# A gated-scan mixer and two local-attention layers on one core: norm shift moved into biases, small steps moved from GpSimd to VectorE and ScalarE, and the loop over passes written out

## The reference

```
q, k = l2norm(q) * qs, l2norm(k) * ksc          # per head, over 64 features
q, k = rotary_xpos(q, k)                        # q*cos*scale + rotate_half(q)*sin*scale, k with 1/scale
x = x + local_attention(q, k, v) @ wo
h = shift_token(x)                              # second half of the features from the token before
h = (h - mu) / jnp.sqrt(var + 1e-05) * lg + lb
a, g = jnp.split(h @ w1 + b1, 2, axis=-1)
x = x + (a * jax.nn.gelu(g)) @ w2 + b2
```

## Time and profile before

| | us |
|---|---|
| median of 3 runs | 432.49 (432.48 to 435.87) |
| span of the profiled execution, first to last instruction | 431.7 |
| TensorE busy | 351.5 (81%) |
| VectorE busy | 321.6 (74%) |
| GpSimd busy | 301.1 (70%) |
| ScalarE busy | 280.8 (65%) |
| weight loads of TensorE, beside its products | 287.5 (67%) |

### The profile page before, as it was taken

One profiled execution on the slowest core, in us unless ns is written; L12 is line 12 of the kernel. 1 busy time (PEld: TensorE's weight loads), 2 busy tenths in 40 slices (PEclk: granted clock), 3 DMA queues, 4 the chain that ended last, 5 costly groups with the idle time before them and its releaser, 6 DMA issues.

```text
span 431.7 us, 11030 instructions
## 1 busy us (share of the span) xinstructions
PE 351.5 (81%) x3832; PEld 287.5 (67%) x3832; DVE 321.6 (74%) x751; ACT 280.8 (65%) x844; POOL 301.1 (70%) x247
## 2 busy tenths in 40 slices
PE   1573055899999899999999999999999989988781
PEld 1352034677778687778777887788778867766561
DVE  6889964787689767966796788688869877954653
ACT  3552263688678677867786788678777868764430
POOL 2200419899999889988998699869887988780222
PEclk9996557999999999999999999999999999998966
DMA  7700042412142125112511342043204220220110
GB/s 262 225 0 0 13 125 60 110 27 50 46 118 56 32 55 141 30 30 64 133 32 33 105 94 51 15 121 76 62 3 117 65 53 2 57 57 2 24 49 25
DMA packets 42373, 28.29 MB, mean 66 GB/s; under 512 B 21668, under 2 KB 36566, under 8 KB 42326
## 3 DMA queue, kind: packets, MB, share of 16 engines
q1 hardware_dynamic: 42325, 27.68, 24.4%
HBM read 13.51 MB, written 3.15 MB: 39 GB/s over the span
## 4 chain that ended last, share of the span: by engine, by line
PE 37%; DVE 23%; POOL 19%; issue 11%; ACT 7%; DMA 1%; SPq 1%; POOLq 1%; DVEq 0%; ACTq 0%
POOL rn L507 7%; PE bank L726 5%; POOL rot L552 4%; PE bank L771 4%; DVE rot_sin L1153 4%; PE upper L708 3%; DVE rot_cos L1153 3%; POOL rot L541 3%; ACT probs L902 3%; PE bank L650 2%; PE bank L763 2%; DVE normed L1052 2%; PE upper L659 2%; PE bank L590 2%; DVE neg_max L1201 2%
## 5 line engine op out<-in xcount | busy, mean ns | idle before, releaser
L902 ACT ACTIVATE probs<-upper,neg_max 128x128 f32<-128x128 f32 x256 | 90.4, 369 | 48.5 <-DVE neg_max L1201 48.4
L507 POOL TENSOR_TENSOR rn<-floored,minus_half 128x16 f32<-128x16 f32 x32 | 93.8, 2930 | 2.7
L541 POOL TENSOR_TENSOR rot<-rot_cos,rot_sin 128x512 f32<-128x512 f32 x32 | 40.9, 1277 | 44.3 <-issue 23.6
L1201 DVE TENSOR_REDUCE neg_max<-upper 128x4 f32<-128x512 f32 x64 | 43.1, 684 | 27.5 <-PE upper L708 27.4
L552 POOL TENSOR_TENSOR rot<-rot,rn 128x1024 f32<-128x1024 f32 x32 | 60.9, 1903 | 2.5
L902 ACT ACTIVATION_READ_ACCUMULATOR probs<-upper,neg_max 128x1 f32 x256 | 53.0, 207 | 0.0
L590 PE MATMUL bank<-wqkv_hi,act_t_hi 128*128 128x512 f32 x96 | 43.3, 452 | 7.9 <-DVE act_t_lo L1140 2.8
L1153 DVE TENSOR_TENSOR rot_cos<-bank,tab 128x512 f32<-128x512 f32 x64 | 43.6, 681 | 2.0 <-PE bank L594 1.9
L1153 DVE TENSOR_TENSOR rot_sin<-bank,tab 128x512 f32<-128x512 f32 x64 | 43.4, 679 | 0.0
L542 POOL TENSOR_TENSOR rot<-rot_cos,rot_sin 128x512 f32<-128x512 f32 x32 | 40.9, 1279 | 0.0
L1160 DVE TENSOR_REDUCE ss<-sq 128x16 f32<-128x1024 f32 x32 | 38.7, 1209 | 2.4 <-ACT sq L944 2.3
(11 more groups left out here) (140 smaller groups left out, 863.7 us busy)
## 6 DMA issues: line engine op xcount, KB each, us to landing
v_mid<-v_tok SPq DMA_DIRECT2D x64, 128.0 KB, 2.3
tab_raw<-tables SPq DMA_DIRECT2D x8, 512.0 KB, 3.4
h_tok<-group_in SPq DMA_DIRECT2D x14, 128.0 KB, 3.5
x_res<-group_in SPq DMA_DIRECT2D x28, 64.0 KB, 1.8
wqkv_raw<-wqkv SPq DMA_DIRECT2D x2, 768.0 KB, 6.8
x_in<-x SPq DMA_DIRECT2D x4, 256.0 KB, 3.6
head_scale<-head_scales SPq DMA_DIRECT2D x8, 128.0 KB, 4.0
group_in<-normed SPq DMA_DIRECT2D x4, 256.0 KB
```

What stands on the lines that cost most here:

```text
L507: pool.tensor_tensor(rn[:, 0:2 * HEADS], floored[:, 0:2 * HEADS], minus_half[:, :], ALU.pow).then_inc(rn_ready, 1)
L541: pool.tensor_tensor(rot[cur.par][:, :, 0:32], rot_cos[:, :, 0:32], rot_sin[:, :, 32:64], ALU.add).then_inc(rot_added, 1)
L902: last = act.activation(probs[:, h, :], s_bank[half][:, (h % 4) * P:(h % 4 + 1) * P], ACT.Exp, bias=neg_max[a.par][:, h:h + 1], accum_out= ...
L1201: dve.tensor_reduce(neg_max[a.par][:, 4 * half:4 * half + 4], src, AX.X, ALU.max, negate=True).then_inc(max_ready, 1)
```

## The change

1. The shift `ln_b` of the norm before the feed-forward leaves the activation of h. Instead `w1^T ln_b` is computed once, by 12 one-column products on TensorE after the mixer, and 12 activations on ScalarE add it to `b1`. With the shift gone, the full copy `h2_t` goes too: `h2_lo` is made by one VectorE instruction that reads PSUM, scales, and subtracts `h2_hi`. TensorE now waits for `h2_lo` before the second half of the first chunk and no longer after it.
2. The floor of the sums of squares leaves GpSimd: `ss` gets a second column that holds the floor, and VectorE takes a maximum over the pair right after `sum_squares`.
3. The carry of 64 keys leaves GpSimd for ScalarE, which takes them straight from PSUM at j = 1.
4. `scale_table` of groups 1 to 7 leaves GpSimd for VectorE, at the end of each position (the four slots of group 0 stay on GpSimd).
5. `place_early` moves from the end of `finish_group` (j = 2) to behind `rotate` of j = 3.
6. All passes are written out; `Fori`, register-valued waits and `settle` are gone.

```diff
-        ss = sb("ss", [P, 2 * HEADS])
+        ss = sb("ss", [P, 2 * HEADS, 2])
...
+        def passes(body, ending):
+            for G in range(-1, LAST - 1):
+                body(G)
+            body(LAST - 1, 2)
             ending()
...
+            pool.memset(ss[:, :, 1], NORM_FLOOR).then_inc(init_done, 1)
...
             def norm_roots(t):
-                pool.wait_ge(ss_ready, t + 1)
-                settle(pool)
-                pool.tensor_scalar(floored[:, 0:2 * HEADS], ss[:, :], NORM_FLOOR, None, ALU.max).then_inc(ss_floored, 1)
+                need(pool, rot_scaled, t)
                 pool.wait_ge(ss_floored, t + 1)
...
-                    if not (number and not 0 <= G < LAST - 1):
-                        scale_table(G + 1, j)
...
-                    if cur.valid and cur.slot == 0 and not (number and G < 0):
-                        pool.wait_ge(k_saved, t)
-                        pool.wait_ge(s_done, 2 * (t - GT + 1))
-                        settle(pool)
-                        if cur.first:
-                            pool.memset(k_t[:, :, 0:WINDOW], 0.0).then_inc(k_carried, 1)
-                        else:
-                            pool.tensor_copy(k_t[:, :, 0:WINDOW], k_t[:, :, GTOK:GTOK + WINDOW]).then_inc(k_carried, 1)
...
+            def project_shifts():
+                pe.wait_ge(w_ffn_in, W_IN)
+                pe.wait_ge(hidden_read, GROUPS)
+                for l in range(DEPTH):
+                    pe.wait_ge(w_big_in[l], 32)
+                    for part in range(2):
+                        for c, (c0, cn) in enumerate(CHUNKS):
+                            at = 6 * l + 3 * part + c
+                            last = pe.matmul(shift_bank[0:cn, at:at + 1], w1_raw[l][:, part * HID + c0:part * HID + c0 + cn],
+                                             lngb[l][:, 1:2], start=True, stop=True)
+                last.then_inc(shift_up, 1)
...
                         if c == 0 and part == 1:
                             if between:
                                 between()
-                            pe.wait_ge(h2t_saved, 2 * F + 2)
-                            settle(pe)
+                            pe.wait_ge(h2_split, F + 1)
                         pe.matmul(b[0:cn, :], w1_hi[layer][:, w], h2_hi[:, :], start=True, stop=False)
                         pe.matmul(b[0:cn, :], w1_lo[layer][:, w], h2_hi[:, :], start=False, stop=False)
-                    if c == 0:
-                        pe.wait_ge(h2_split, F + 1)
-                        settle(pe)
...
+            def shift_biases():
+                act.wait_ge(shift_up, 1)
+                for l in range(DEPTH):
+                    for part in range(2):
+                        for c, (c0, cn) in enumerate(CHUNKS):
+                            at = 3 * part + c
+                            act.activation(b1_sb[l][0:cn, at:at + 1], shift_bank[0:cn, 6 * l + at:6 * l + at + 1], ACT.Identity,
+                                           bias=b1_sb[l][0:cn, at:at + 1]).then_inc(bias_ready, 1)
...
+            def carry_keys(a):
+                if tile(a.t + 1).first:
+                    source = zeros[:, 0:WINDOW].unsqueeze(1).broadcast_to([P, PAIRS, WINDOW])
+                else:
+                    source = kt_bank[:, :].rearrange("p (c t) -> p c t", c=PAIRS)[:, :, P - WINDOW:P]
+                act.copy(k_t[:, :, 0:WINDOW], source).then_inc(k_carried, 1)
...
-                act.activation(dst[:, :], h2t_bank[:, :], ACT.Identity, bias=lngb[l][:, 1:2],
-                               scale=lngb[l][:, 0:1]).then_inc(h2t_saved, 1)
+                act.activation(h2_hi[:, :], h2t_bank[:, :], ACT.Identity, scale=lngb[l][:, 0:1]).then_inc(h2t_saved, 1)
...
+            def scale_table(G, j):
+                dve.wait_ge(tab_in, 32 * (G + 1))
+                dve.tensor_tensor(tab[:, j, :], tab_raw[:, j, :], head_scale[:, :], ALU.mult).then_inc(tab_ready, 1)
...
-                dve.tensor_reduce(ss[:, :], sq[:, :].rearrange("p (h d) -> p h d", h=2 * HEADS), AX.X, ALU.add).then_inc(ss_ready, 1)
+                dve.tensor_reduce(ss[:, :, 0], sq[:, :].rearrange("p (h d) -> p h d", h=2 * HEADS), AX.X, ALU.add).then_inc(ss_ready, 1)
+                dve.wait_ge(ss_ready, a.t + 1)
+                need(dve, rn_ready, a.t)
+                dve.tensor_reduce(floored[:, 0:2 * HEADS], ss[:, :, :], AX.X, ALU.max).then_inc(ss_floored, 1)
...
-                dve.wait_ge(h2t_saved, 2 * (F + 1))
-                dve.tensor_tensor(h2_lo[:, :], h2_t[:, :], h2_hi[:, :].bitcast(F32), ALU.subtract).then_inc(h2_split, 1)
+                dve.wait_ge(h2t_saved, F + 1)
+                dve.scalar_tensor_tensor(h2_lo[:, :], h2t_bank[:, :], lngb[F // GROUPS][:, 0:1], h2_hi[:, :].bitcast(F32),
+                                         ALU.mult, ALU.subtract).then_inc(h2_split, 1)
...
             def finish_group(F, layer):
                 sum_group(F, layer, x_attn)
-                dve.wait_ge(carry_in, 16 * (F + 1))
-                place_early(F + 1)
...
                     if cur.valid:
                         rotate(cur)
+                    if j == 3 and G >= 1:
+                        dve.wait_ge(carry_in, 16 * G)
+                        place_early(G)
...
+                    if 0 <= G < LAST - 1:
+                        scale_table(G + 1, j)
```

More of the change, by code:

```diff
@@ L259, in tile @@
[L259 to L280 removed]
+            if value > 0:
+                eng.wait_ge(s, value)
@@ L299, in link @@
                 self.catch_up()
-            def enter(self):
-                self.start, self.n = self.base + self.n, 0
-            def at(self, i, each):
-                self.base, self.each = self.start + i * each, each
-            def leave(self, times):
-                assert self.n == self.each, f"a pass of the loop has {self.n} steps"
-                self.base, self.n = self.start + times * self.each, 0
         def low_pieces(l):
@@ L384, in load_carry @@
                 need(sp, h2_in, 64 * (F + 1))
-                ends = isinstance(F, int) and F % GROUPS == GROUPS - 1
+                ends = F % GROUPS == GROUPS - 1
                 last = zeros[P - 1:P, 64:128] if ends else x_attn[P - 1:P, GT, 64:128]
-                dst = x_last if isinstance(F, int) and F == LAST - 2 else x_attn
+                dst = x_last if F == LAST - 2 else x_attn
                 sp.dma_start(dst[P - 1:P, 0, 64:128], last).then_inc(carry_in, 16)
@@ L399, in store @@
                     sp.dma_start(by_group(out)[F - GROUPS], y_out[:, :, :]).then_inc(stored, 16)
-                if not (isinstance(F, int) and F == LAST - 1):
+                if F != LAST - 1:
                     need(sp, carry_in, 16 * (F + 1))
@@ L449, in body @@
                         load_carry(G - 1)
-                    if j == 3 and number and G > GROUPS + 1:
+                    if j == 3 and G > GROUPS + 1:
                         store(G - 2, DEPTH - 1)
-                if count == GT and not (number and (G < 1 or G > GROUPS)):
-                    store(G - 1, (G - 1) // GROUPS if number else layer)
+                if count == GT and 1 <= G <= GROUPS:
+                    store(G - 1, (G - 1) // GROUPS)
             def ending():
@@ L787, in body @@
                 for j in range(count):
-                    cur, prev, mid, done, after = (At(G, j, back, layer) for back in range(5))
-                    ffn = j == 2 and not (number and G < 1)
+                    cur, prev, mid, done, after = (At(G, j, back) for back in range(5))
+                    ffn = j == 2 and G >= 1
                     if cur.valid:
@@ L807, in body @@
                         pe.wait_ge(k_saved, prev.t + 1)
-                    if j == 0 and not (number and not 0 <= G < LAST - 1):
+                    if j == 0 and 0 <= G < LAST - 1:
                         transpose_inputs(G + 1)
@@ L1225, in place_early @@
             def place_early(G):
-                if not (isinstance(G, int) and G >= LAST - 1):
+                if G < LAST - 1:
                     dve.wait_ge(xa_ready, GT * G + 2)
@@ L1254, in normalise_out, with body @@
                 last.then_inc(y_normed, 1)
-            def body(G, layer, count=GT):
-                number = isinstance(G, int)
+            def body(G, count=GT):
                 for j in range(count):
-                    cur, prev, mid, done, after = (At(G, j, back, layer) for back in range(5))
-                    norm, ffn = (j == n and not (number and G < 1) for n in (1, 2))
-                    final = j == 3 and number and G > GROUPS
+                    cur, prev, mid, done, after = (At(G, j, back) for back in range(5))
+                    norm, ffn = (j == n and G >= 1 for n in (1, 2))
+                    final = j == 3 and G > GROUPS
                     if mid.valid and j != 3:
```

190 lines of the change are left out of this document (75 added, 115 removed).

## The result

| | before | after |
|---|---|---|
| median, us | 432.49 (4 runs, 431.75 to 435.87) | 416.07 (4 runs, 414.75 to 417.01) |
| span of the profiled execution | 431.7 | 413.5 |
| TensorE busy | 351.5 | 352.9 (85%) |
| VectorE busy | 321.6 | 338.5 (82%) |
| GpSimd busy | 301.1 | 271.9 (66%) |

The ratio is 0.9598, with a 95% interval of 0.9557 to 0.9638. The change is faster by 16.4 us. The gain of 12.3 that I summed was a quarter too small.

What follows compares the result with a forecast made beforehand. No engine owned the chain; GpSimd's L552 gated TensorE, which had 2.0 us idle per pass. Gains 7.8 + 2.1 + 1.3 + 0.6 + 0.6 + 0.3 - 0.4 = 12.3 gave span 419.4, median 420.2, range 415.5 to 427.

Steps and rivals of the forecast that it cites:

- Rival (c): TensorE's L650 waits for GpSimd move to L681, leaving a gain of about 4 less 1: 429.5 us, chance 0.06.
- Rival (d): VectorE waits for the head scales at j = 0, each microsecond late costing seven: 441 us, chance 0.03.
- The feed-forward stretch: Passes 1 to 6, from j = 2: 1.3 us gained per pass with refilling, 7.8 in all.
- Pass 0: The pass without feed-forward, nearly bound by GpSimd: 1.3 us gained.
- rival (a): TensorE loses all 2.0 us idle per pass and pass 0 falls to its floor: 16.3 gained, 416, chance 0.12.
- the loop: Writing out the two passes still in the hardware loop gains 0.6 us.
- The 0.3 lost on VectorE at j = 1: VectorE gets 0.65 us more work at j = 1 against 0.35 of wait, so 0.3 stays.
- The GpSimd part of the stretch: At j = 2, L650's gate and L733's wait for h go: 0.7 us per pass, with refilling 0.8.
- h_lo: It starts after the first activation and takes 0.75 instead of 1.05: 0.5 us per pass with refilling.
- The gate at j = 0: L650 at j = 0 loses its gate of 0.22 and its refill: 0.3 us, seven times, 2.1 in all.
- The port rule: VectorE instructions with two SBUF inputs contend with GpSimd: 2.2 us of gain lost, 422.3; left out of the sum.
- rival (b): VectorE's 0.65 at j = 1 counts in full and the scaling collides at j = 2: 4.3 less, 425, chance 0.2.

Runs made afterwards that it cites:

- Experiment 8: The kernel after, with GpSimd's power on 4 columns instead of 16 and one column scaling every head: 412.57 us, ratio 0.9519.
- Experiment 9: The kernel after, with each table slot scaled a second time on VectorE into a tile nobody reads: 425.71 us, ratio 0.9822.
- Experiment 7: The kernel after, with table scaling, floor and key carry all back on GpSimd: 429.89 us, ratio 0.9928.
- experiment 5: The kernel after, with part 1 undone, the shift back in two activations of h: 419.94 us, ratio 0.9659.
- Experiment 11: The kernel before, passes written out, with only the table scaling of groups 1 to 7 moved to VectorE: 427.40 us, ratio 0.9855.
- experiment 1: The kernel before, with only the passes and the store loop written out: 433.80 us, ratio 1.0008.
- experiment 4: The kernel after, with `place_early` back in `finish_group`: 418.10 us, ratio 0.9635.
- experiment 6: The kernel after, with the key carry back on GpSimd: 416.49 us, ratio 0.9606.
- experiment 10: The kernel after, with unread TensorE products added, 24 in the prologue and 14 before the last feed-forward: 413.80 us, ratio 0.9555.
- experiment 3: The kernel after, with the floor of the sums of squares back on GpSimd: 421.80 us, ratio 0.9728.
- experiment 12: The kernel after, with unread products: 34 in the prologue, 8 and 16 short ones around the first tiles, 14 before the last feed-forward: 411.93 us, ratio 0.9508.

## Why the prediction was right about the cause and short on the size

**Right: what bounded the kernel, and what would go.** GpSimd's L552 gated TensorE, and this change takes the gate away. GpSimd's busy time fell by 29.2. I had said some 33, but its powers and second additions together grew by 2.9 beside VectorE's scaling (95.6 and 42.0 after, 93.8 and 40.9 before). L650's waits vanished but for the first, and on VectorE `row_max` at j = 2 and `h` no longer wait; at j = 0 `row_max` still waits 1.13 (pass 5). Rival (c), that L681 would wait in their place, is out: the transposes of probs come earlier by all that was gained. Rival (d) is out: VectorE never waited for the head scales.

**The step that failed: the refill and the cover in "The feed-forward stretch" and "Pass 0".** I wrote that TensorE had 2.0 us a pass to give and took 1.3 and 0.3 of it. The passes between tiles 14 and 26 lost 2.0 each, and rival (a)'s 16.3 is near the 16.2 that came. The number is partly luck: rival (a) had all of the idle time go, and in fact 0.5 of it stays and 0.56 of busy time went in its place. Experiment 8 shows that GpSimd is out of the balance, since 1.9 us less GpSimd work at each position changes no step. What is left is TensorE's own work, and VectorE beside it for 8.6 us of each pass.

From 12.3 to 16.2, the steps of the table above add 2.1 in the feed-forward steps, 1.4 from j = 0 to 1, 0.7 from j = 3 to 0, 0.5 in pass 0 and 0.4 for the y statistics; the loop, the start and the step from j = 1 to 2 take back 0.6, 0.5 and 0.1. The feed-forward stretch is the term most out of size: 1.3 a pass forecast, 1.6 to 1.7 measured. By terms:

- *The 0.3 lost on VectorE at j = 1* didn't exist. I set 0.65 of added work against a wait of 0.35. In fact `row_max` starts 2.87 after `sum_squares` as before: the two instructions cost 0.12 + 0.10 + 0.34 = 0.56 instead of 0.65, and the statistics of h give back 0.12, since their aggregation now starts 0.90 after their start, not 1.02 (VectorE's timelines). The 0.44 that stays is what the wait of 0.35 and the gap at its end had held. Experiment 9 shows how close this was: 0.31 more, and 0.30 arrives.
- *The GpSimd part of the stretch*, 0.8 with refilling. Experiment 7 puts it at 1.0 to 1.2 with part 1 in place, and together with part 1 it is more still. The 0.8 had the 0.3 of VectorE taken off; with that back it would have been 1.1.
- *`h_lo`*, 0.5: too large, 0.30 (experiment 5). The parts sum to 1.3 forecast against 1.6 to 1.7 measured, since 0.3 more comes only when both are done. Experiment 11 gives a hint, as with the old `h_lo` part of what `rot` no longer holds up is lost to a longer wait for `h_lo`; these 0.3 weren't tried separately.
- *The gate at j = 0*, 0.3 each: 0.34 to 0.39 at tiles 18, 22 and 26, and 0.8, 0.5 and 0.8 at tiles 10, 14 and 30. I had taken the row of one pass for all. Experiments 1 and 11 speak for GpSimd's weight split as the extra at tiles 10 and 14: it stays without the loop, and 0.3 of it stays with the tables gone (9.00 against 8.68). The split itself wasn't taken out.
- *Output roots*, 0.6: 0.6 in the feed-forward step of pass 6 and 0.3 in the one after it.
- *Pass 0*, 1.3 and 0.3: 2.1; TensorE is busy 32.32 of 33.03.
- *Loop*, 0.6: 0.1 (experiment 1). The row was read rightly, 42.60 against 42.07, and its cause wrongly.
- *y statistics*, -0.4: nothing was lost. Pass 5 takes 40.10 with them. The 1.81 of cover was enough.
- *Start*, 0.3: -0.2, inside the scatter of that start.

Together these make 16.2 by tile 30, of which 12.3 was forecast. The other 2.0 of the profiled difference lie in the ending, which no term of mine treated. The last feed-forward of both kernels begins after an idle TensorE, at 1.2 GHz: before for 5.3 us (412.83 to 418.1), after for 2.7 (396.33 to 399.06). Experiments 4 and 6, whose edits leave the ending's program as it is, took 47.6 and 47.2 for it, and the table under experiment 10 shows that the granted clock goes with the length whatever the edit. So the 2.0 is luck of one execution for the most part. The medians differ by 16.4 and the ratio gives 17.4, so 0.2 to 1.2 us lie outside the 16.2 of the start and the passes; whether the edits cause them is not shown.

**The port rule** would have given 422.3. (With the 2.2 as written it is 422.4.) The contention is there (experiments 3, 9 and 11), but the change keeps clear of it where it would count: at j = 2 the scaling costs 0.47 instead of 0.39. My first reason for leaving it out was half wrong. The scaling falls on `pow` only at j = 1, and takes 0.39 there. At j = 0 and 3 it starts in the second addition and takes 0.87 and 0.54 (j = 0 of pass 5, j = 3 of pass 4), and `pow` is slowed too. That 0.87 is over the 0.6 that I had named as the sign of rival (b). It cost nothing, since VectorE still waits 0.63 behind it at j = 0 and 1.13 behind the 0.54.

## What to carry to other kernels

When several edits all shorten the engine that gates the bound one, the gain ends near the bound engine's own work. Here its idle time per pass (2.0) was a better forecast than a sum of careful refills. The same parts are worth more when made first than when undone last (5.9 and 3.1 for the tables), so price the set, not its members. Before more work goes to an engine "with room", look for the position where it has none, and see what its instruction runs beside.

## What the runs showed of the hardware

**VectorE and GpSimd slow each other, and `pow` is not spared.** VectorE's 128 x 256 product with both inputs in SBUF takes 0.39 where no GpSimd addition runs, even inside a GpSimd power, and 0.47, 0.87 and 1.50 where it starts 0.19, 0.59 and 1.21 before the end of a GpSimd addition. In all three it ends 0.28 to 0.29 after the addition does, as if it had waited for it: what sets the price is how far the addition still has to go. GpSimd's 16-column power takes 2.91 where the scaling starts 0.64 into it (j = 1 of pass 5), and more where the scaling is under way as it starts. In the kernel after, at j = 0 of pass 5, GpSimd and then VectorE:

```profile
284.58 3.09 POOL L457 TENSOR_TENSOR rn<-floored,minus_half 128x16 f32<-128x16 f32 x1
```

```profile
284.03 0.87 DVE L1122 TENSOR_TENSOR tab<-tab_raw,head_scale 128x256 f32<-128x256 f32 x1
```

In experiment 3, where the scaling starts 0.01 after it, it is 3.19. The Trainium skill names the shared interfaces in "GPSIMD Engine Reference", section 1, Specifications, for VectorE instructions with two SBUF inputs. The runs agree and give the size, 0.1 to 1.1 us for one instruction.

**Unread products paid for themselves.** TensorE's granted clock was 1.2 GHz after its idle times at the start and in the ending, and products of 512 columns then came 0.43 apart instead of 0.23. Filling those times brought 2.2 us in the ending (experiment 10, against the shortest ending without them) and 3.1 at the first tile (experiment 12), of which 2.3 is left at tile 30. In experiment 12 both together are 0.9% of the kernel by the ratios. Its five runs spread over 1.3 us; the four of experiment 10 spread over 3.2, so a narrower scatter is not shown for the ending's products alone. "TensorE: Matmul & The Clock Gate" of the Trainium skill, Part 1, says that the throttled state is the default and that activity releases it, and these runs agree.
